# Two transformer layers on one core: the loop over eight pairs of sequences written out, and the last pair without a lookahead

## The reference

```python
x = L0_attn_hidden_states                      # (16, 512, 256)
x = x + _L0_attn_ref(_layernorm(x), w_q, w_k, w_v, w_o)     # softmax in blocks of 256 keys, each with its own maximum
x = x + _L0_ffn_ref(_layernorm(x), ...)        # relu(x W)^2 W', ternary weights, a low-rank term
x = x + _L1_attn_ref(_layernorm(x), qkv_w, qkv_b, out_w, out_b)
x = x + _L1_ffn_ref(_layernorm(x), W_in, b_in, W_out)       # 8 decision trees of 255 nodes
```

## Time and profile before

| | us |
|---|---|
| median of 3 runs | 3482.56 (3480.83 to 3483.92) |
| profiled execution, its own time | 3486.33 |
| span of the profiled execution | 3484.4 |
| first exponential of pair 1, of pair 2 | 592.39, 1005.5 |
| branches of PE's loop, first and last | 587.1 and 3482.3 |
| granted clock of TensorE, mean | 0.937 |

### The profile page before, as it was taken

How to read it: one execution, slowest core, us unless ns; L and a number is a source line. 1 busy time by engine, 2 the same in 40 slices (tenths; PEclk the granted TensorE clock), 3 DMA queues, 4 the chain that set the end, 5 groups by cost and what they waited for, 6 DMA issues and landing times.

```text
span 3484.4 us, 58777 instructions
## 1 busy us (share of the span) xinstructions
PE 3057.5 (88%) x19068; PEld 1364.6 (39%) x19068; DVE 2249.3 (65%) x4159; ACT 1933.7 (55%) x2573; POOL 917.2 (26%) x1216
## 2 busy tenths in 40 slices
PE   0488899989999899888999889998999889988899
PEld 0124254242633336342452425424263333634245
DVE  0784856757566666757667485666756666675766
ACT  0274654737556474655647465473755647465563
POOL 0013223141321424123231322314132131412323
PEclk9589999989999899998999999998998989989899
DMA  3000000000100001000010000100010000100001
GB/s 114 21 21 19 21 26 33 20 19 21 40 27 11 29 23 38 27 10 30 14 44 21 19 21 26 36 18 19 21 43 25 10 29 24 37 27 11 29 14 43
DMA packets 95781, 94.36 MB, mean 27 GB/s; under 512 B 16185, under 2 KB 92889, under 8 KB 95465
## 3 DMA queue, kind: packets, MB, share of 16 engines
q1 hardware_dynamic: 95477, 90.44, 7.6%
HBM read 18.53 MB, written 8.39 MB: 8 GB/s over the span
## 4 chain that ended last, share of the span: by engine, by line
issue 67%; POOL 19%; PE 7%; DVE 3%; SPq 2%; ACT 1%; POOLq 1%; DMA 0%; DVEq 0%; ACTq 0%
POOL probs L416 5%; POOL parts L357 4%; POOL probs L378 3%; PE ps L975 2%; SPq L263 2%; PE ps L1020 2%; POOL rstd L353 1%; PE ps L1191 1%; POOL x L373 1%; POOL nres L365 1%; POOL x L387 1%; POOL npart L367 1%; POOL npart L363 1%; POOL npart L369 1%; PE ps L1220 1%
## 5 line engine op out<-in xcount | busy, mean ns | idle before, releaser
L519 ACT ACTIVATE probs<-ps 128x1024 f32<-128x1024 f32 x1024 | 1043.5, 1026 | 414.3 <-PE ps L1031 406.6
L1020 PE MATMUL ps<-kst,qst 48*128 48x512 f16 x2076 | 761.4, 416 | 195.6 <-DVE nmax L741 61.1
L741 DVE TENSOR_REDUCE nmax<-ps 128x2 f32<-128x512 f32 x1052 | 667.2, 684 | 256.3 <-PE ps L1020 251.5
L744 DVE TENSOR_REDUCE nmax<-ps 128x1 f32<-128x512 f32 x1024 | 649.9, 684 | 242.1 <-PE ps L1020 240.7
L1031 PE MATMUL ps<-qst,kst 54*128 54x512 f16 x2048 | 720.2, 411 | 5.0 <-ACT probs L519 5.0
L1042 PE MATMUL ps<-probs,vn 128*32 128x512 f32 x4096 | 544.7, 605 | 7.8 <-ACT oT L507 7.8
L1020 PEld LDWEIGHTS ps<-kst,qst 48*128 48x128 f16 x2076 | 158.9, 94 | 888.0 <-DVE nmax L741 392.0
L416 POOL TENSOR_TENSOR probs<-probs 127x512 f16<-127x512 f32 (+1 forms) x256 | 292.3, 1163 | 521.8 <-ACT probs L644 521.8
L644 ACT ACTIVATE probs<-probs 127x512 f16<-127x512 f32 (+1 forms) x256 | 161.3, 630 | 359.9 <-DVE probs L931 355.0
L975 PE MATMUL ps<-hT,win 128*127 128x512 f16 (+1 forms) x1536 | 354.3, 380 | 5.0 <-ACT probs L620 5.0
L1220 PE MATMUL ps<-wout,probs 127*128 127x256 f16 (+1 forms) x3072 | 357.3, 273 | 0.0
(11 more groups left out here) (115 smaller groups left out, 3240.6 us busy)
## 6 DMA issues: line engine op xcount, KB each, us to landing
qst<-parts SPq DMA_DIRECT2D x396, 64.0 KB, 2.6
kst<-parts SPq DMA_DIRECT2D x396, 64.0 KB, 2.6
x<-in_x SPq DMA_DIRECT2D x18, 512.0 KB, 4.6
probs<-x SPq DMA_DIRECT2D x16, 512.0 KB, 3.0
out<-probs SPq DMA_DIRECT2D x16, 512.0 KB, 3.0
qst<-nrow SPq DMA_DIRECT2D x258, 12.0 KB
qst<-in_winT SPq DMA_DIRECT2D x1, 2040.0 KB
oT<-in_wfcT SPq DMA_DIRECT2D x1, 1024.0 KB
```

The costliest lines, as they stand in the source:

```text
L519: nc.scalar.activation(probs[:, g % 2, 2 * hf:2 * hf + 2, s % G, :], ps[:, 2 + 2 * hf:4 + 2 * hf, :], ACT.Exp).then_inc(exp_rd, 1)
L741: nc.vector.tensor_reduce(nmax[:, u, 2 * tt + half, :, slot], bank[tt % 2].rearrange("p (a s) -> p a s", s=BLK), AX.X, ALU.max, negate=Tru ...
L744: nc.vector.tensor_reduce(nmax[:, u, 2 * tt + half, 0, slot:slot + 1], bank[tt % 2], AX.X, ALU.max, negate=True).then_inc(max_rd, 1)
L1020: mm(bank[tt % 2], qst[lo:hi, ai % 2, e // 2, tt * P:(tt + 1) * P], kst[lo:hi, ai % 2, e // 2, :], start=True, stop=True).then_inc(max_ps, 1)
```

## The change

All five loops become Python loops (`for b in range(PAIRS)`), so that the program holds the body eight times. There are no loop counters and branches left, and each wait has a constant as its target. A flag `more` is false for the last pair. Where it is false, the lookahead is left out on all engines: the loads of the next pair, its moments and norms, its transposes, queries, keys and values, the 28 tiles of maxima, and the splits, rows and transfers that belong to them. The final waits of SyncE are lowered by what is no longer issued.

```diff
                 sp.wait_ge(x_kept[q], b * 16 + 16)
-                load(q, (b + 1) % PAIRS)
+                if b + 1 < PAIRS:
+                    load(q, b + 1)
...
-            with sp.Fori(0, PAIRS) as b:
+            for b in range(PAIRS):
+                more = b + 1 < PAIRS
...
-            with dve.Fori(0, PAIRS) as b:
+            for b in range(PAIRS):
+                more = b + 1 < PAIRS
...
+                    if more and a == 6:
                         arrived(b + 1, 0)
                         moments(b + 1, 0)
-                    if a == 7:
+                    if more and a == 7:
                         normalise(b + 1, 0)
...
-            with pe.Fori(0, PAIRS) as b:
+            for b in range(PAIRS):
+                more = b + 1 < PAIRS
...
-                    if a == 8:
+                    if more and a == 8:
                         transposed(b + 1, 0, 0)
                         transposed(b + 1, 0, 1)
-                    if a == 9:
+                    if more and a == 9:
                         hT_read(b + 1, 0, 0)
                         hT_read(b + 1, 0, 1)
                         qk_unit(n4, 0, 0)
...
                 tree_sum(b, TREES - 2)
-                lead_tiles(n4, 0, 11)
+                if more:
+                    lead_tiles(n4, 0, 11)
                 pe.wait_ge(masked_sb, b * (2 * TREES) + 2 * TREES)
-                maxima_rows(n4, 0)
+                if more:
+                    maxima_rows(n4, 0)
                 tree_sum(b, TREES - 1)
-                lead_tiles(n4, 0, 12)
-                lead_tiles(n4, 0, 13)
+                if more:
+                    lead_tiles(n4, 0, 12)
+                    lead_tiles(n4, 0, 13)
                 pe.wait_ge(x_upd, (b + 1) * (2 * PHASES))
```

More of the change, by code:

```diff
@@ L339, in _ @@
             for q in range(PAIR):
[L340 to L342 removed]
+                sp.wait_ge(x_in[q], 16 * PAIRS)
+                sp.wait_ge(stack[q], (16 * 4 * SLOTS) * (PAIRS * NATT))
+            sp.wait_ge(mstack[0], 64 * PAIRS * NATT)
         @block.gpsimd
@@ L462, in _ @@
                     leaf_low(b, a)
-                    if a == 14:
+                    if more and a == 14:
                         split_maxima(n4, 0, 0)
@@ L917, in _ @@
                         tree_residual(b, 0)
-                    if a == 10:
+                    if more and a == 10:
                         arrived(b + 1, 1)
                         moments(b + 1, 1)
-                    if a == 12:
+                    if more and a == 12:
                         lead_tiles(0)
-                    if a > 12:
+                    if more and a > 12:
                         lead_tiles(2 + 3 * (a - 13))
@@ L933, in _ @@
                             actv[0:rows, a % 2, leaf, :], ALU.is_equal, ALU.mult).then_inc(masked_sb, 1)
-                    if a == 10:
+                    if more and a == 10:
                         normalise(b + 1, 1)
-                    if a >= 12:
+                    if more and a >= 12:
                         lead_tiles(1 + 3 * (a - 12))
-                lead_tiles(11)
+                if more:
+                    lead_tiles(11)
                 tree_residual(b, 1)
-                lead_tiles(12)
-                lead_tiles(13)
+                if more:
+                    lead_tiles(12)
+                    lead_tiles(13)
         @block.tensor
@@ L1371, in _ @@
                         qk_unit(n4, 0, 0)
-                    if a == 10:
+                    if more and a == 10:
                         pe.wait_ge(qk_sb, n4 * 4 + 1)
                         v_unit(n4, 0, 0)
-                    if a == 11:
+                    if more and a == 11:
                         pe.wait_ge(v_sb, n4 * 2 + 1)
                         qk_unit(n4, 0, 2)
-                    if a >= 13:
+                    if more and a >= 13:
                         lead_tiles(n4, 0, 2 + 3 * (a - 13))
```

40 lines of the change are left out of this document (20 added, 20 removed).

## The result

| | before | after |
|---|---|---|
| median of the runs, us | 3483.24 (3480.83 to 3484.15, 4 runs) | 3437.68 (3437.46 to 3438.51, 4 runs) |
| ratio after to before | | 0.9871, 95% interval 0.9854 to 0.9888 |
| profiled execution and its span, us | 3486.33, 3484.4 | 3437.46, 3435.4 |
| first exponential of a pair to that of the next, us, pair 0 to 1 | 418.31 | 413.47 |
| the same, pairs 1 to 7 | 411.87 to 415.72 | 409.52 to 409.65 |

The change is faster, by 45.6 us (1.3%). The forecast was 49.3 us, 3433.3 us as a time, and the measured time lies 4.4 us above it and inside its range. The forecast of the span, 3435.1 us, met the 3435.4 more closely than it deserved: the profiled execution of before was 3.1 us above its median, and one of its pairs took 415.72 us where its neighbours took some 412 or 413.

The account below looks back on a forecast made before the run. PE was taken as the bound, busy 3057.5 of 3484.4 us. Branches 27.3, clock 2.8, registers 0 and lookahead 19.2 sum to 49.3 us, off the median 3482.56: 3433.3 us, range 3405 to 3446.

Parts of the forecast that it names:

- The bound, PE's gaps for `issue`: Between pairs: PE bounds the kernel and idles 28.3 us in 7 waits ended by nothing the profile knows; these should vanish.
- Part 1, branches: At the seven pair boundaries: without the taken branch each stretch moves up 3.90 us, 27.3 us in all; bounds 24 and 28.
- Part 1, which engine: At pair boundaries: PE's stall counts, ScalarE's of about 2 us is hidden behind it, VectorE's branch is recorded with 63 ns.
- The clock's 2.8 us: Start of each pair's first phase: clock falls some 3 us into the phase, not before; 0.4 us per boundary, 2.8 in all.
- Part 2, registers: Waits in all phases: constants instead of registers save 0; bounds 0 and 10 us.
- Part 3, lookahead: Last pair's tree steps: without lookahead they come 5.65 us apart on PE, saving 19.2 us; bounds 15 and 20.
- The clock stays up: Rival, start of a pair: the shorter gap no longer makes the clock fall; 4.0 us more each, 28, time 3405; chance 0.14.
- The stall stays, at another place: Rival: PE also waits for the written-out program once per pair, only part 3 is left, 3463.4 us; chance 0.08.
- starves the engines: Rival: engines must fetch the whole written-out program; two stalls per pair cost 62 us, giving 3495.5; chance 0.03.
- Another engine holds the last steps: Rival, last pair: tree steps take 6.43 us rather than 5.65, part 3 loses 6.2 us, time 3439.5; chance 0.08.

Follow-up runs that it names:

- the second trace of before: The kernel before, unchanged, run and profiled once more; 3482.57 us over 10 runs.
- the first experiment: Against the kernel before: all five loops written out, the last pair's lookahead kept; 3457.94 us against 3483.13, ratio 0.9928.

## Why the prediction was right, point by point

- **The bound, PE's gaps for `issue`.** Right. They fell from 7 to none, and a kernel with six or three branches shows six or three of them.
- **Part 1, branches: 27.3 us.** Somewhat too large, at 25.2. The term took VectorE's idle time of 3.90 us as gone as a whole, with the first tile at the upper clock (0.39 us). At pair 0 to 1 just that happened: VectorE has no gap there. At the other six boundaries the clock has fallen ahead of the tile, which takes 0.58 us, and VectorE waits 0.17 us for it; at pair 1 to 2, 3.61 us go. That is 1 us of the 2.1. The rest goes with phase 0, which has become longer: it takes 52.4 us where the second trace of before has 52.17 in the mean; of the clock's time at the lower level 15.6 us now lie behind the first exponential, and 14.2 to 15.5 did there. The lower bound of the prediction, 3.4 each for "one of the other waits at this place", was nearer than its centre. First exponentials were to lie 4.3 us closer together; from pair 1 on they lie 3.3 us closer in the mean, against the second trace of before. The transfer of rows of maxima was not late, as worked out.
- **Part 1, which engine.** Right in sum, incomplete in cause. The prediction had PE's stall, ScalarE's hidden under it and a cheap branch on VectorE; VectorE has a stall too, and the longer one covers the other. Since the change removes all, it made no difference, which was luck; for a change at PE alone the sum would have been twice the truth.
- **The clock's 2.8 us.** Wrong. The step was that the clock falls some 3 us into the phase. It does so at pair 0 to 1 only, 1.9 us into it. What that is worth was about right: step 15 to the first exponential takes 18.12 us there and 18.34 or 18.35 at the others, and phase 0 takes 52.25 for 52.42, 0.4 us together. At the other six it falls ahead of the phase's first tile; ahead of the first of these falls PE was busy for 2.24 of 3.40 us. So one boundary brought what each of the seven was to bring. The argument had set the busy time of a stretch between 1.29 us, after which the clock fell, and 2.33, after which it stayed; in a later experiment it fell after 2.39, so such a comparison could not carry it. Together with the item above that makes 25.2 of 30.1.
- **Part 2, registers: 0.** Right; the loop of two pairs per pass leaves 0.9 us for them.
- **Part 3, lookahead: 19.2.** Right. From step 7's start to the span's end it went from 80.09 to 60.57 us, 19.5 less; against the first experiment, which has no branches either, it is 79.7 to 60.57, 19.1. Steps 0 to 7 take 43.6 us with and without the lookahead. So the chain of `logits`, `select` and `tree_sum` was read rightly, and step 7 to 8 lost its 0.62 us of idling for silu and more: 5.65 for 6.43 us. By the medians the lookahead is worth 20.3. The two traces differ by another 1.2 us in pair 0, which takes 414.67 us in the first experiment and 413.47 in the changed kernel, half of it in the first phase, where the two programs are the same; that is no part of the last pair.
- **Rivals.** *The clock stays up* did not come about by itself: with the branch gone the clock still falls. Its price (28 us) was in the right region: holding it up in phase 0 by force, at the cost of extra work, brought 21.3. The rule of the Trainium skill's "TensorE: Matmul & The Clock Gate", Why this matters for your kernels, that it is the long gaps that matter, was not enough here: 0.87 and 0.96 us were the longest gaps in the stretches ahead of two of the falls, and both are short. *The stall stays, at another place* and *starves the engines* are out: no `issue` wait of PE in the written-out kernels. *Another engine holds the last steps* is out by the 5.65 us.
- **What the stall is.** The prediction supposed the wait for the instructions at the target. The Trainium skill, "Runtime: NRT & Kernel Launch", Instruction fetch mechanics, says as much: a taken branch to a page that isn't held forces a fetch. The runs bear out what goes with it: the stall stands behind taken branches alone, on TensorE, VectorE and ScalarE, and never in straight-line code. But GpSimd and SyncE go back after about 0.2 us, and no run here varied the body's size, so the fetch itself is argued and not shown.

## What to carry to other kernels

Look for idle time ended by nothing and count it: if there is one such wait per pass, a loop's branch is the first suspect. Writing the loop out for the engine that bounds and for the one that it waits for next brought nearly all of it back here (24.3 of 25.2 us). When a stall goes, subtract the waits that take its place (3.6 of 3.9 us were left), and look for a second stall under the first in the idle times of the other engines, not in the records of their branches. A peeled last pass was worth what its lookahead cost the engine that bounds the end, and here it added to the rest.

## What the runs showed of the hardware

- A taken branch at the end of such a loop: 3.9 us on PE (28.3 us of idling in 7 waits), 2.74 to 2.96 us to the next record on VectorE, 2.33 to 2.64 on ScalarE and about 0.2 on GpSimd and SyncE. The branch's own record shows only PE's.
- Pairs that differ by 2 us in length with the loop and by 0.1 without it; what differs is chiefly whether the clock falls once more between the second and the third phase.
- The clock fell after stretches in which PE was busy for 2.24 and 2.39 of 3.40 us, and stayed at the lower level for 20.50 us while PE was busy for all of them. With the same instructions in the loop the third phase kept it in four pairs and lost it in four.
- A phase that starts at the upper level and keeps it takes 48.78 us with its extra work in it, against 52.42 without; work that was added for nothing but the clock shortened the kernel by 42.7 us. It costs where the clock is low already: 2.3 us in pair 0, and the same additions in the kernel with its loops made that one 26 us slower.
